# Attention and quantized FFN on one core: the bias store on GpSimd's queue, loads, sums and list entries moved

## The reference, cut to what matters

```python
Q, K, V = (proj(Wq), proj(Wk), proj(Wv))            # per batch, 16 heads of 8
att = einsum('bhqd,bhkd->bhqk', Q, K) * (1 / sqrt(8)) + b[0]
att = att * m + (1.0 - m) * NEG_INF                 # m: the mask over keys
y = einsum('bhqk,bhkd->bhqd', softmax(att), V)      # back to (B, C, T)
h = silu(bit_linear(y, w_gate)) * bit_linear(y, w_up)   # 256 -> 1024
h = rms_norm(h, ln_weight)
out = x + bit_linear(h, w_down)                     # 1024 -> 256
```

## Time and profile before

| what | us |
|---|---|
| median of 3 runs (162.35 to 163.65) | 163.2 |
| the profiled execution | 163.05 |
| its span, first to last instruction | 161.2 |
| TensorE busy | 143.8 |
| VectorE busy | 136.7 |
| ScalarE busy | 125.4 |
| GpSimd busy | 104.0 |

### The profile page before, as it was taken

The page is one execution under the profiler, slowest core; times in us unless marked ns, Lnnn a source line. Parts: engine busy times, 40 slices in busy tenths (PEclk is TensorE's granted clock), DMA queues, the critical chain, the costliest instruction groups (busy, mean ns, idle before and its releaser), DMA issues.

```text
span 161.2 us, 4126 instructions
## 1 busy us (share of the span) xinstructions
PE 143.8 (89%) x1402; PEld 66.7 (41%) x1402; DVE 136.7 (85%) x204; ACT 125.4 (78%) x255; POOL 104.0 (65%) x185
## 2 busy tenths in 40 slices
PE   6968998998999999999997999979889966999893
PEld 2644553433333333433333333332323342665672
DVE  6788998898999989789997999993398788999972
ACT  3042377899899899989889889886999966998970
POOL 5889625848818818806898997822313579689920
PEclk9999999999999999999999999999999999999999
DMA  3994896457255345533233000000000000001012
GB/s 107 278 206 97 262 294 191 141 141 213 71 135 147 85 108 173 192 76 82 62 74 86 3 3 4 5 5 4 3 0 4 0 0 2 0 33 39 33 65 98
DMA packets 19904, 14.19 MB, mean 88 GB/s; under 512 B 2360, under 2 KB 18800, under 8 KB 19884
## 3 DMA queue, kind: packets, MB, share of 16 engines
q1 hardware_dynamic: 16940, 11.52, 25.7%
q10 hardware_dynamic: 2624, 2.17, 5.2%
q0 software_dynamic: 320, 0.25, 1.0%
HBM read 6.17 MB, written 1.07 MB: 45 GB/s over the span
## 4 chain that ended last, share of the span: by engine, by line
PE 55%; DVE 12%; ACT 11%; POOL 8%; issue 7%; DMA 4%; SPq 1%; ACTq 0%; DVEq 0%; POOLq 0%
PE y_ps L1073 14%; PE s_ps L1034 13%; ACT probs L570 5%; PE t_ps L1053 5%; DVE maxes L944 4%; PE s_ps L1164 4%; PE t_ps L1006 3%; DMA bias_scr<-bias_parts 2%; PE t_ps L1094 2%; ACT hid_sq L675 2%; PE y_ps L1114 2%; PE t_ps L1183 2%; PE t_ps L1015 2%; DVE hid L878 2%; PE t_ps L1203 2%
## 5 line engine op out<-in xcount | busy, mean ns | idle before, releaser
L944 DVE TENSOR_REDUCE maxes<-s_ps 128x4 f32<-128x1024 f32 x64 | 76.0, 1218 | 6.8 <-PE s_ps L1034 6.6
L570 ACT ACTIVATE probs<-t_ps 128x512 f32<-128x512 f32 x118 | 65.9, 591 | 8.6 <-PE t_ps L1053 6.2
L1034 PE MATMUL s_ps<-k_st,q_st 64*128 64x256 bf16 x256 | 44.7, 274 | 1.0 <-DMA k_st<-bias_scr 0.5
L1053 PE MATMUL t_ps<-q_st,k_st 64*128 64x256 bf16 x236 | 42.5, 274 | 3.3 <-ACT probs L570 1.6
L1073 PE MATMUL y_ps<-probs,v_pad 128*18 128x256 f32 x512 | 38.6, 384 | 0.2 <-ACT probs L570 0.2
L1034 PEld LDWEIGHTS s_ps<-k_st,q_st 64*128 64x128 bf16 x256 | 15.8, 94 | 29.6 <-issue 16.0
L1164 PE MATMUL s_ps<-w_q,ffn_x 128*128 128x512 bf16 x64 | 17.2, 380 | 2.9 <-DVE hid L878 2.4
L523 POOL TENSOR_TENSOR hw<-hid,ln_bc 128x512 f32<-128x512 f32 x8 | 10.2, 1273 | 12.0 <-DVE hid L867 8.9
L1053 PEld LDWEIGHTS t_ps<-q_st,k_st 64*128 64x128 bf16 x236 | 14.0, 94 | 8.3 <-ACT probs L570 3.6
L438 POOL TENSOR_SCALAR nm_parts<-maxes 128x16 bf16<-128x16 f32 x16 | 3.3, 207 | 21.6 <-DVE maxes L944 21.5
L1073 PEld LDWEIGHTS y_ps<-probs,v_pad 128*18 128x18 f32 x512 | 9.6, 96 | 14.2 <-issue 11.6
(11 more groups left out here) (116 smaller groups left out, 245.6 us busy)
## 6 DMA issues: line engine op xcount, KB each, us to landing
q_st<-parts SPq DMA_DIRECT2D x48, 64.0 KB, 2.7
k_st<-parts SPq DMA_DIRECT2D x33, 64.0 KB, 2.4
w_f<-in_wgT ACTq DMA_DIRECT2D x2, 512.0 KB, 4.7
w_f<-in_wuT SPq DMA_DIRECT2D x2, 512.0 KB, 4.3
w_f<-in_wdT SPq DMA_DIRECT2D x2, 512.0 KB, 4.9
out<-o_sb SPq DMA_DIRECT2D x8, 128.0 KB, 1.7
k_st<-parts ACTq DMA_DIRECT2D x15, 64.0 KB, 3.1
x_sb<-in_x SPq DMA_DIRECT2D x2, 256.0 KB, 3.9
```

The costliest lines, as they stand in the source:

```text
L570: act.activation(probs[:, t % NP_RING].rearrange("p e t -> p (e t)"), src, ACT.Exp, scale=SCALE)\
L944: dve.tensor_reduce(dst[:, :, s, :], s_ps[:, c % 2], AX.X, ALU.max).then_inc(s_maxed, 1)
L1034: mm = pe.matmul(s_ps[:, c % 2, i, e, :], q_st[b % RING][rows, hp, qt * P:qt * P + P], k_st[b % RING][rows, hp, :], start=True, stop=True)
L1053: mm = pe.matmul(t_bank(bank["t", t])[:, e * T:e * T + T], k_st[b % RING][rows, hp, kt * P:kt * P + P], q_st[b % RING][rows, hp, :], start ...
```

## The change

- The store of the bias is issued on GpSimd's queue, behind the seventh bias instruction, and no longer on SyncE's. GpSimd makes the identity matrices ahead of the bias instead of behind it.
- SyncE loads x of batches 5 to 7 behind the bias rows of stack 0, and the first two half matrices of weights around it: one ahead of it, one behind the parts of stack 1. ScalarE loads neither.
- The fourth stack is cleared by GpSimd, at the end of round -1; what waits for it waits for a semaphore of its own.
- The first two weight sums stand one step earlier.
- The last four filler products ahead of the first scores are gone.
- The steps of the weights' rounding are spread over rounds 4 to 7.
- In the FFN tail VectorE takes unit 5's product ahead of `normalize_y(7)`, the scale of batch 1 and the maximum of batch 2 behind unit 6's product, and the scale of batch 2 behind unit 7's; ScalarE copies batch 0's transposed hidden ahead of the squares of batch 3.

```diff
--- before.py
+++ after.py
@@ -32,7 +32,7 @@
 LATE_T_BANKS = (0, 3, 4)
 LATE_BANKS = (2, 1)
 INTS_SLOT = (5, 3)
-WEIGHT_SUM_SLOTS = {(-1, 5): 0, (-1, 7): 1, (0, 6): 2, (1, 6): 3, (2, 6): 4, (3, 3): 5}
+WEIGHT_SUM_SLOTS = {(-1, 4): 0, (-1, 6): 1, (0, 6): 2, (1, 6): 3, (2, 6): 4, (3, 3): 5}
 WEIGHT_TOTAL_SLOT = (3, 5)
 EARLY = (("qk", 1), ("v", 0), ("qk", 2), ("v", 1), ("v", 2), ("qk", 3))
 AHEAD = 3
@@ -211,6 +211,7 @@
 
         q_zeroed = sem("q_zeroed")
         k_zeroed = sem("k_zeroed")
+        last_zeroed = sem("last_zeroed")
         v_zeroed = sem("v_zeroed")
         ident_ready = sem("ident_ready")
         bias_step = sem("bias_step")
@@ -303,6 +304,8 @@
         def load_high(queue, b, side):
             if b >= RING:
                 queue.wait_ge(unit_ready, unit["t", 16 * (b - RING + 1) - 1] + 1)
+            elif b == RING - 1:
+                queue.wait_ge(last_zeroed, 2)
             elif b:
                 queue.wait_ge(q_zeroed, b + 1)
                 queue.wait_ge(k_zeroed, b + 1)
@@ -357,16 +360,16 @@
             load_mask(sp, 1)
             load_rows(0)
             load_x(2)
-            load_x(3)
             load_high(sp, 0, 0)
-            sp.wait_ge(bias_step, 7)
-            sp.dma_start(bias_scr, bias_parts[:, :, :, :].to_broadcast([B, 2, 3, T])).then_inc(bias_stored, 16)
             load_low(sp, 0, (0,))
             load_bias(0)
+            load_weights(sp, 0)
+            load_x(3)
             load_rows(1)
             load_bias(1)
             load_high(sp, 1, 0)
             load_low(sp, 1, (0,))
+            load_weights(sp, 1)
             load_mask(sp, 2)
 
             for n in range(FIRST, LAST + 1):
@@ -403,6 +406,11 @@
             pool.memset(ident_b[:, :], 0.0).then_inc(ident_ready, 1)
             pool.memset(ident_f[:, :], 0.0).then_inc(ident_ready, 1)
 
+            pool.wait_ge(ident_ready, 2)
+            for m in (ident_b, ident_f):
+                pool.affine_select(out=m[:, :], in_=m[:, :], compare_op=ALU.not_equal, fill=1.0,
+                                   base=0, pattern=[[-1, P]], channel_multiplier=1).then_inc(ident_ready, 1)
+
             pool.wait_ge(mask_in, 32)
             pool.tensor_scalar(bias_t[:, 0, :], mask8[:, :], -1.0, NEG / SCALE, ALU.add, ALU.mult).then_inc(bias_step, 1)
             pool.tensor_scalar(bias_t[:, 1, :], mask8[:, :], b8[:, 0:1], 1.0 / SCALE, ALU.mult, ALU.mult)\
@@ -419,10 +427,8 @@
             pool.tensor_tensor(bias_parts[:, 0, 2, :], bias_t[:, 2, :], bias_parts[:, 0, 1, :], ALU.subtract)\
                 .then_inc(bias_step, 1)
 
-            pool.wait_ge(ident_ready, 2)
-            for m in (ident_b, ident_f):
-                pool.affine_select(out=m[:, :], in_=m[:, :], compare_op=ALU.not_equal, fill=1.0,
-                                   base=0, pattern=[[-1, P]], channel_multiplier=1).then_inc(ident_ready, 1)
+            pool.wait_ge(bias_step, 7)
+            pool.dma_start(bias_scr, bias_parts[:, :, :, :].to_broadcast([B, 2, 3, T])).then_inc(bias_stored, 16)
             pool.memset(ones_f[:, :], 1.0).then_inc(small_const, 1)
             pool.memset(half_neg[:, :], -0.5).then_inc(small_const, 1)
 
@@ -485,8 +491,7 @@
             def load_constant_rows(b):
 
                 if b < RING:
-                    pool.wait_ge(q_zeroed, b + 1)
-                    pool.wait_ge(k_zeroed, b + 1)
+                    pool.wait_ge(last_zeroed, 2)
                     pool.dma_start(q_st[b % RING][BIAS_ROWS], ones6[:, :, :].to_broadcast([6, NHP, T]))\
                         .then_inc(later_rows_in[b % RING], 16)
                 else:
@@ -498,7 +503,7 @@
                                bias_scr[b].rearrange("i k t -> (i k) t").unsqueeze(1).to_broadcast([6, NHP, T]))\
                     .then_inc(later_rows_in[b % RING], 16)
 
-            weight_steps = {4: ((), (0, 1)), 5: ((2, 3), (4, 5)), 6: ((6, 7), (8,))}
+            weight_steps = {4: ((), (0, 1)), 5: ((2, 3), (4,)), 6: ((5,), (6,)), 7: ((7, 8), ())}
             split_parts(1)
             for n in range(FIRST, LAST + 1):
                 if has(n):
@@ -511,6 +516,10 @@
                     negate_maxes(n + 1, 0)
                 if n >= 0 and has(n + 3):
                     load_constant_rows(n + 3)
+                if n == -1:
+                    pool.memset(q_st[RING - 1][:, :, :].rearrange("p h t -> p (h t)").bitcast(f32), 0.0).then_inc(last_zeroed, 1)
+                    pool.memset(k_st[RING - 1][:, :, :].rearrange("p h t -> p (h t)").bitcast(f32), BF16_ONES)\
+                        .then_inc(last_zeroed, 1)
                 for step in weight_steps.get(n, ((), ()))[1]:
                     quantize_weights(step)
 
@@ -645,8 +654,6 @@
             load_high(act, 1, 1)
             copy_qk(3)
             load_low(act, 1, (1,))
-            for q in range(2):
-                load_weights(act, q)
             act.wait_ge(k_zeroed, 3)
 
             def tanh_unit(u):
@@ -741,11 +748,11 @@
             hidden_mean(AHEAD - 1)
             silu_unit(2 * AHEAD + 1)
             for b in range(AHEAD, B):
+                if b == AHEAD:
+                    take_hidden_t(0)
                 if b < B - 1:
                     square_hidden(b)
                     hidden_mean(b)
-                if b == AHEAD:
-                    take_hidden_t(0)
                 if b == AHEAD + 1:
                     copy_last_ints()
                 if b + 1 < B:
@@ -786,7 +793,7 @@
             dve.tensor_copy(lot[:, :, 1, :], qk_r[:, :, :]).then_inc(parts_step, 1)
             dve.wait_ge(parts_step, 2)
             dve.tensor_tensor(lot[:, :, 2, :], qk_r[:, :, :], lot[:, :, 1, :], ALU.subtract).then_inc(parts_step, 1)
-            for r in range(1, RING):
+            for r in range(1, RING - 1):
                 clear_stacks(r)
 
             def mean_weights():
@@ -954,24 +961,26 @@
                             gate_times_up(u)
                         if u == 2:
                             hidden_maximum(0)
-                        if u == 4:
+                        if u == 5:
                             normalize_y(B - 1)
-                        if u == 5:
                             weight_high_half(2)
-                            hidden_steps(1)
                     if s in (4, 8):
                         weight_high_half(s // 4 - 1)
                     if s == 8:
                         hidden_steps(0)
                         hidden_maximum(1)
 
-            hidden_maximum(AHEAD - 1)
             for b in range(AHEAD, B):
                 gate_times_up(2 * b)
-                hidden_steps(b - 1)
+                if b == AHEAD:
+                    hidden_steps(1)
+                    hidden_maximum(AHEAD - 1)
+                else:
+                    hidden_steps(b - 1)
                 gate_times_up(2 * b + 1)
                 weight_high_half(b)
                 if b == AHEAD:
+                    hidden_steps(AHEAD - 1)
                     scale_y(B - 1)
                     scale_late_tokens()
                 if has(b - 4):
@@ -1130,7 +1139,6 @@
             project_v(2)
             keep_array_busy(2)
             project_qk(3)
-            keep_array_busy(4)
 
             def gate(u):
                 b, f = divmod(u, 2)
```

## The result

The changed kernel takes 164.96 us (median of 20 runs, 163.20 to 166.54), the kernel before 163.21 us beside it on the same chips (20 runs, 162.33 to 165.53). The ratio is 1.0092, 95% interval [1.0065, 1.0120]: slower by 0.9%, where 162.05 us, within 160.9 to 163.5, was predicted. The profiled execution took 165.08 us (span 163.3), 2.1 us more than the one of before.

The account below looks back on a forecast made before the run. It took a chain of transfers, with SP's issue time nearly a bound, to limit the head, and DVE to pace the tail. Head 0.45 + tail 0.7 = 1.15 us off 163.05 gave 161.9, as median 162.05; range 160.9 to 163.5.

Parts of the forecast that it names:

- Store, masks, first scores: Head: bias store lands at 11.2 instead of 12.53, masks cost nothing, first scores at 13.6 to 13.65, 1.25 us earlier.
- gap of 0.82: Head, GpSimd's queue: unexplained 0.82 us of idleness before its first own transfer, counted into the store's landing at 11.2.
- rival 1: Head: SP's queue not late or first-time gap absent; head 1.0 to 1.3 us, whole 161.3; chance 0.25.
- T: Head: landing time of the bias store, taken as 11.2, bounds 10.4 and 12.7; first exponential starts at T + 15.1.
- Rival 3: Head: store lands late, held up by DVE, 165.7 us; or masks start slowly, 163.2; chance 0.12.
- SP's queue gives most of it back: Head, SP's queue: added loads cost 1.45 us of issue, so rows of maxima go out at 23.94, only 0.12 earlier.
- Head: 0.45 us: Head: first exponential at about 26.3 instead of 26.8, gain 0.45 us; bounds 1.3 earlier, 1.0 later.
- second sum: Head, ACT: second weight sum ends at 24.4, no longer holding the first exponential.
- x and the weights' rounding: Head and later rounds: x's 0.55 us stall is hidden; spreading the rounding gives 0, bounds -0.2 and +0.2.
- Memsets: 0: Head: GpSimd clearing the fourth stack costs 0, bounds 0 and 1.8 us; without the move first maxima would hardly start sooner.
- The tail: 0.7: FFN tail, DVE: new order cuts idleness from 1.71 to 0.91 us, gain taken as 0.7.
- bound of -0.4: FFN tail: lower bound of its gain, if GpSimd, rounding batch 1 some 0.3 us later, is late with the next limits.

Follow-up runs that it names:

- b3: Changed kernel with the four dropped filler products restored and eleven more where TensorE waits for the rows of maxima; 164.65 us, ratio 1.0109.
- d3: c2 with both weight loads on SyncE's queue; 163.70 us, ratio 1.0018.
- a2: Changed kernel with the old FFN lists of DVE and ACT; 164.97 us, ratio 1.0131.
- a3: Changed kernel with eight filler products where TensorE waits for the rows of maxima; 164.82 us, ratio 1.0113.
- c3: Changed kernel with x of batches 5 to 7 loaded early on SyncE again, before the first stack; 165.32 us, ratio 1.0129.
- a1: Changed kernel with the first two weight loads back on ACT's queue; 162.96 us, ratio 1.0017.
- a4: Kernel before with only the new FFN lists on DVE and ACT; 163.85 us, ratio 1.0034.
- b2: Changed kernel with both weight loads on ACT and both old FFN lists; 163.38 us, ratio 1.0027.
- c1: a1 with DVE's late scales ahead of batch 2's steps; 163.82 us, ratio 1.0030.
- c2: Changed kernel with the fourth stack's memsets on DVE, both weight loads on ACT and both old FFN lists; 162.52 us, ratio 0.9961.
- d1: c2 with the new FFN lists of DVE and ACT; 163.24 us, ratio 1.0004.
- d2: d1 with the four late 128x2 scale operations written as pairs of one column each; 162.82 us, ratio 0.9966.
- b4: b2 with ACT's FFN list as changed; 163.63 us, ratio 1.0015.
- b1: Changed kernel with only the second weight load moved back to ACT's queue; 163.52 us, ratio 1.0047.

## Why the prediction was wrong, point by point

- **Store, masks, first scores: right.** Landing predicted 11.2, measured 10.88; scores 13.6 and 13.32. The "gap of 0.82" was 0.31, so rival 1 was partly true, though T stayed above its 10.4 to 10.7. Rival 3 did not come in its size. Whether the store was held at all is open: in all fourteen executions with it, it starts 0.01 to 0.02 us after DVE's second cast ends (here 7.50 to 8.28), but also always 0.30 to 0.31 after the last bias instruction, so the rows can't tell the two apart. Behind that only a subtraction and memsets of DVE ran beside it, no cast. The 6 us that the Trainium skill's page "GPSIMD Engine Reference" (section "Instruction dispatch") gives for a first call of a freshly loaded routine did not show either: the masks took 0.28 each. But no row shows that a routine was freshly loaded here, so this trace does not test it, and the prediction's "does not agree" said too much.
- **"SP's queue gives most of it back": right in kind, mis-sized, and this is the first step that failed.** From the bias read to the rows of maxima I summed 11.24 + 1.45 = 12.69 us; it took 24.73 - 10.89 = 13.84, 1.15 more. I had priced each added load at its own 0.49 us of issue. At 18.79 nine of the stacks' parts (64 KB each) asked for since 15.36 had not landed, and the issue took 1.31 more than the 0.44 of the first load's; the six parts ahead of it took 0.54 more than before (4.35 instead of 3.81), and the last three 0.62 less (1.86 instead of 2.48). The long issue is not the weight load's own: in b3 it fell on the mask (1.67 us), in d3 on a stack part, in a2 on ACT's queue as well. My own row had one in it: the 2.48 for three parts hold one of 1.20, where a part takes about 0.6. With both loads on SyncE's queue (after, a2, a3, b3, c3, d3) each head has an issue of 1.2 us or more; with both on ACT's, none does in a1, a4, b2, c1, c2, d1 and d2, and the kernel before does. Rows at 23.94 were forecast; with T at 10.88 they would have been at 23.6.
- **"Head: 0.45 us": not there.** The two profiled executions give -0.39, of which a4 leaves the sign open; with the loads on ACT it is +0.9 (a1). And the second sum, said to be out of the way at 24.4, ended at 24.95 since its load landed 4.99 us after it was asked for.
- **Clock: not in the sum at all, the second step that failed and the dearer one.** I took a later TensorE start as worth its own length. Idleness of TensorE can cost more than itself: 0.8 us in round 0, 0.6 to 0.7 in the tail, 1.5 of the 2.1 us. The kernel before had 0.49 us of idleness in round 0; I never asked what would follow at five times that.
- **x and the weights' rounding: right.** TensorE shows no stall for x, and its wait in round 5 is 0.84 us against 0.86.
- **"Memsets: 0": right for their cost, wrong for their worth.** I wrote that without them "the maxima would hardly start sooner". True, but c2 shows that the exponential does not need the maxima sooner.
- **"The tail: 0.7": wrong.** The idleness went from 1.71 to 1.18 (0.53 gained), and the held scale took 0.75 back. The bound of -0.4 held this 0.23 loss; the clock behind it was outside.
- **Term by term.** Against the forecast the profiled execution lost 0.84 in the head, 0.80 to the clock in round 0, 0.93 in the tail and 0.70 behind it: about 3.2 us in all (165.08 against 161.9). With the two loads back on ACT the time is 162.96, inside the range given, so the loads and the clock behind them are what carried it out. That a1 lies there is in part luck: its head is better than forecast and its tail worse.
- **Rivals.** No rival had either mechanism. The slower one was put on the store, whose landing was the part that worked.

The Trainium skill describes a hold of the kind met in the tail: its page "SBUF — State Buffer" (section "Who interferes with whom") says that a DVE operation with both inputs in SBUF, or a one-source one that runs in a two-port mode, shares GpSimd's access, and that whoever issues first holds it for the whole instruction. These traces agree: 0.98 instead of 0.23, 1.30 instead of 0.69, and 1.64 instead of 1.12 the other way round. That the 128x2 scale runs in a two-port mode no row shows; d2 shows only that one column at a time it is not held. I had used that section for the transfer alone.

**What stays open.** Why an issue stretches is not known. Nine parts were outstanding at 18.79, but this does not decide it: over the traces other than b4's, 65 of 1,590 issues of parts, masks and weights took over 1.0 us (outstanding counted by the landings in the traces), some with a single transfer outstanding (1.63 us in b1 at 35.70), and of the 19 with ten or eleven outstanding none did. c3 moved too much at once to help. Why the clock fell behind some stretches of idleness and not behind others as long is open too. Whether the old tail's two outcomes alternate from run to run of one kernel is likely from the medians of b2 and c2, but only profiled executions show which was met. c2's and d2's lead over the kernel before, 0.4% and 0.3%, is near what the measurement can tell: their intervals end at 0.9995 and 0.9999.

## What to carry to other kernels

- An issue has no fixed price: here 0.44 us in one place and 1.75 in another for the same load. Before moving a large load ahead of a small transfer that an engine waits for, ask where the small one stands, and leave large loads on a queue whose next item is not urgent.
- Ask of every new idleness on TensorE what the clock may do behind it: here 1 us of idleness cost up to 1.5 more, and 2 us at times nothing more.
- When DVE's list is moved, look for GpSimd instructions beside its two-input and one-source SBUF operations. An idle gap removed can be paid back as a hold, and the one-column form escaped it here.
- Take a package apart before judging it. Of this one, the store with x behind it (and the small moves left in c2) gives 0.4% at best; the weight loads and the FFN lists take it away.

## What the runs showed of the hardware

- TensorE's granted clock fell from 2.4 to 1.2 GHz for 3.4 us at a time, behind idleness of 2.58, 2.00, 1.05 (twice), 1.02 and 0.77 us before the first transposed scores and of 2.1 us before c3's first scores. It did not behind 1.00 (a1) and 0.61 (b2) at the first place, nor behind 1.26 before a4's first scores. In the tail it fell behind 1.96 us (after, d1; within 0.02 of it in a1, a3, b1 and b3) and 1.72 (d2), and not behind 1.97 (a4, c3). So the length of one idle stretch did not decide it. It varies over executions of one kernel too: two of the 20 timed ones of the changed kernel had the full clock over the whole span.
- A small store on GpSimd's queue landed 2.5 to 2.6 us after its issue in the twelve profiled executions (without b4's) in which the last 384 KB of x stood behind it, and 4.6 us in c3, the one with them ahead, on SyncE's queue.
- Issues on SyncE's and ACT's queues that mostly take 0.4 to 0.6 us took 1.0 to 2.0 in 65 of 1,590 cases, with one to nine transfers outstanding.
- DVE and GpSimd held each other: a DVE scale of 128x2 took 0.98 us instead of 0.23 beside a GpSimd rounding of 128x1024, and 0.34 for the pair when written as two of 128x1.
